# A fused decoder layer, its attention stage in another order: the context's maximum asked for between two query products, column sums one K/V tile later, the next batch element's transposes among the queries, the last products ahead of the layer norms

## What is computed

```
# 1: linear attention through one vector A per batch element
Xn = layernorm(x) * gamma + beta
Q, K, V = split(Xn @ W_in + b_in)
K, V = rotary(K), rotary(V)
A = 0.5 * sum over positions (K/|K| * V/|V|) + 0.5
x1 = layernorm(x + (A * Q) @ W_out + b_out + x)
# 2: product with ctx, both quantised to fp8 and back, scale = 448 / max|.|
x2 = layernorm(x1 + fp8(x1) @ fp8(ctx) + mask)
# 3: gated MLP (512 -> 2048 -> 512) plus 8 retrieved experts per token
out = layernorm(x2 + mlp(x2) + experts(x2))
```

## Time and profile before

| | us |
|---|---|
| median of 3 runs | 868.43 (864.55 to 869.49) |
| profiled execution: its own time | 864.76 |
| profiled execution: span of the instructions | 863.0 |
| TensorE busy | 790.3, 92% of the span |
| VectorE busy | 687.5, 80% |
| ScalarE busy | 298.0, 35% |
| GpSimd busy | 388.6, 45% |

### The profile page before, as it was taken

How to read it: one execution, slowest core, us unless ns; L and a number is a source line. 1 busy time by engine, 2 the same in 40 slices (tenths; PEclk the granted TensorE clock), 3 DMA queues, 4 the chain that set the end, 5 groups by cost and what they waited for, 6 DMA issues and landing times. The chain is left out here.

```text
span 863.0 us, 10406 instructions
## 1 busy us (share of the span) xinstructions
PE 790.3 (92%) x3510; PEld 639.1 (74%) x3510; DVE 687.5 (80%) x1329; ACT 298.0 (35%) x657; POOL 388.6 (45%) x308
## 2 busy tenths in 40 slices
PE   4988899998826899899999999999999999999994
PEld 3867688886704667688888888888877887887783
DVE  5658479874878687317777999999999999999997
ACT  5343335451134423221135342333333333333320
POOL 0231222221155423111247766776766766766431
PEclk9989899998965999999999999999999999999998
DMA  9464442576034202200002323232243233322113
GB/s 325 187 128 121 87 105 71 101 247 119 0 94 129 67 19 74 98 25 1 29 28 72 86 85 84 72 88 72 56 125 92 73 110 93 93 85 60 44 60 136
DMA packets 49510, 78.54 MB, mean 91 GB/s; under 512 B 17487, under 2 KB 26447, under 8 KB 48944
## 3 DMA queue, kind: packets, MB, share of 16 engines
q1 hardware_dynamic: 25600, 48.57, 16.7%
q0 software_dynamic: 22272, 29.29, 15.2%
q10 hardware_dynamic: 1584, 0.01, 0.1%
HBM read 107.29 MB, written 12.58 MB: 139 GB/s over the span
## 5 line engine op out<-in xcount | busy, mean ns | idle before, releaser
L1014 POOL TENSOR_TENSOR h_lo<-mid,h_hi 128x512 fp32r<-128x512 f32 x62 | 79.5, 1302 | 117.2 <-ACT h_hi L1134 112.3
L1144 ACT ACTIVATE gates<-dots 128x1 f32<-128x1 f32 x144 | 29.2, 203 | 232.1 <-DVE dots L1350 232.1
L1035 POOL DMA_INDIRECT ctx_q<-table_dram,row_i x64 | 80.6, 1259 | 62.0 <-DVE xall L1359 37.8
L1465 PE MATMUL gu<-x_hi,gate_hi 128*128 128x512 f32 x256 | 102.1, 399 | 3.2 <-DVE mid L1259 1.7
L1035 POOL DMA_INDIRECT scratch<-table_dram,row_i x64 | 82.7, 1293 | 39.5 <-issue 21.3
L1467 PE MATMUL gu<-x_hi,gate_lo 128*128 128x512 f32 x256 | 100.4, 392 | 0.0
L1466 PE MATMUL gu<-x_lo,gate_hi 128*128 128x512 f32 x256 | 100.4, 392 | 0.0
L1467 PE MATMUL gu<-x_hi,up_lo 128*128 128x512 f32 x256 | 99.6, 389 | 0.0
L1465 PE MATMUL gu<-x_hi,up_hi 128*128 128x512 f32 x256 | 99.6, 389 | 0.0
L1466 PE MATMUL gu<-x_lo,up_hi 128*128 128x512 f32 x256 | 99.6, 389 | 0.0
L1465 PE MATMUL ob<-down_hi,h_hi 128*128 128x512 f32 x248 | 97.5, 393 | 1.0 <-POOL h_lo L1014 1.0
(11 more groups left out here) (209 smaller groups left out, 1714.6 us busy)
## 6 DMA issues: line engine op xcount, KB each, us to landing
stage<-in_ctx SPq DMA_DIRECT2D x7, 1024.0 KB, 5.5
total<-prod POOLq DMA_DIRECT2D x12, 512.0 KB, 4.7
xall<-half_bo POOLq DMA_DIRECT2D x4, 1024.0 KB, 10.4
w_stage<-in_L_ffn_gate_w SPq DMA_DIRECT2D x8, 512.0 KB, 3.3
w_stage<-in_L_ffn_up_w SPq DMA_DIRECT2D x8, 512.0 KB, 3.4
w_stage<-in_L_ffn_down_w SPq DMA_DIRECT2D x8, 512.0 KB, 3.5
x_dram<-xall SPq DMA_DIRECT2D x4, 1024.0 KB, 4.9
x_tok<-x_dram SPq DMA_DIRECT2D x16, 256.0 KB, 3.5
```

The source lines that it names most:

```text
L1014: nc.gpsimd.tensor_tensor(lo[:, c], mid[c][:], hi[:, c].bitcast(F32), ALU.subtract).then_inc(hlo_done, 1)
L1035: nc.gpsimd.indirect_dma_start(rows[k], None, table_dram[:, :], bass.IndirectOffsetOnAxis(ap=row_i[t % 2][:, k:k + 1], axis=0), bounds_che ...
L1144: nc.scalar.activation(gates[:, t % 2, k:k + 1], dots[:, t % 2, k:k + 1], ACT.Silu).then_inc(gate_done, 1)
L1465: nc.tensor.matmul(dst, lhs[0], rhs[0], start=start, stop=False)
```

## The change

No arithmetic changes and no DMA is added. The order on three engines does, with the waits and the PSUM banks that it needs:

- TensorE: `token_sums(b-1)` goes behind K/V tile 1 (was: tile 0), `mix_sums(b-1)` behind tile 2 (was: tile 1). The first two transposes of the next element go ahead of the fourth query. `gather_largest(0)` goes between queries 0 and 1 and `spread(0)` behind query 1 (were: ahead of query 0, and behind it).
- The last element's four attention tiles use all four ob banks (were: two), and `gather_largest(1)` uses ob[2], after a wait for `residual` of tile 0.
- ScalarE: `squares(b, 1)` ahead of `copy_sums`, `high_y` (the high part of A*Q) behind `squares(b, 2)`, the first two scalings of the next x between queries 2 and 3, and for the last element `squares(3, 3)` ahead of query 0.
- VectorE: `multiplier` and `low_y` one K/V tile later; `products(0, 3)` behind the four `low` of the next element; `products(3, 3)` ahead of the four `finish_x1`.

```
# tensor
                     if b:
-                        for k in range(KC):
-                            key_value(b, 0, k)
+                        for i in range(2):
+                            for k in range(KC):
+                                key_value(b, i, k)
                         token_sums(b - 1)
-                        for k in range(KC):
-                            key_value(b, 1, k)
+                    for k in range(KC):
+                        key_value(b, 2, k)
+                    if b:
                         mix_sums(b - 1)
-                    for i in (2, 3):
-                        for k in range(KC):
-                            key_value(b, i, k)
+                    for k in range(KC):
+                        key_value(b, 3, k)
+                    query(b, 0)
                     if b == 1:
                         pe.wait_ge(amul_done, 1)
                         gather_largest(0)
-                    for c in range(KC):
-                        query(b, c)
-                        if b == 1 and c == 0:
-                            spread(0)
+                    query(b, 1)
+                    if b == 1:
+                        spread(0)
+                    query(b, 2)
                     if b == 1:
                         pe.wait_ge(scale_done, 1)
                     if b < LAST:
                         transposes(b + 1, 0)
                         transposes(b + 1, 1)
+                    query(b, 3)
# scalar
                     squares(b, 0)
+                    squares(b, 1)
                     if b:
                         copy_sums(b - 1)
-                    squares(b, 1)
-                    if b:
-                        for c in range(KC):
-                            high_y(b - 1, c)
...
                     squares(b, 2)
+                    if b:
+                        for c in range(KC):
+                            high_y(b - 1, c)
+                    if b == LAST:
+                        squares(b, 3)
                     query(b, 0)
                     query(b, 1)
-                    squares(b, 3)
+                    if b < LAST:
+                        squares(b, 3)
                     query(b, 2)
+                    if b < LAST:
+                        scaled_x(b + 1, 0)
+                        scaled_x(b + 1, 1)
                     query(b, 3)
                     if b < LAST:
-                        for c in range(KC):
-                            high(b + 1, c)
+                        high_x(b + 1, 0)
+                        high_x(b + 1, 1)
+                        high(b + 1, 2)
+                        high(b + 1, 3)
# vector
                         add_kv_bias(b, 1)
                         products(b, 0)
-                        multiplier(b - 1)
-                        for c in range(KC):
-                            low_y(b - 1, c)
...
                     add_kv_bias(b, 2)
                     products(b, 1)
-                    if b == 0:
+                    if b:
+                        multiplier(b - 1)
+                        for c in range(KC):
+                            low_y(b - 1, c)
+                    else:
                         low_wo()
...
+                    if b == LAST:
+                        products(b, 3)
                     if b >= 2:
                         for i in range(TB):
                             finish_x1(b - 2, i)
-                    products(b, 3)
+                    if 0 < b < LAST:
+                        products(b, 3)
...
+                    if b == 0:
+                        products(b, 3)
```

More of the change, by code:

```diff
@@ L330, in high_wo, with scaled_x @@
                     nc.scalar.activation(wo_hi[:].rearrange("p c n -> p (c n)"), stage[0][:], ACT.Copy).then_inc(wo_hi_done, 1)
-                def high(b, c):
+                def scaled_x(b, c):
                     j = KC * b + c
@@ L342, in high @@
                     nc.scalar.activation(xn_hi[:, c], xs[:, c % 2], ACT.Copy).then_inc(hi_done, 1)
+                def high(b, c):
+                    scaled_x(b, c)
+                    high_x(b, c)
                 def squares(b, i):
@@ L489, in scale_row @@
                     dve.wait_ge(amax_b, 2 * k + 1)
-                    own.did(nc.vector.tensor_reduce(arow[0:1, 0:1], ob[1][0:1, P:2 * P], AX.X, ALU.max))
+                    own.did(nc.vector.tensor_reduce(arow[0:1, 0:1], scale_bank[k][0:1, P:2 * P], AX.X, ALU.max))
                     own.wait()
@@ L546, in residual @@
                     dve.wait_ge(xb_in, 16 * (b + 1))
-                    nc.vector.scalar_tensor_tensor(tile(j), tile(j), 2.0, ob[2 + i % 2][:], ALU.mult, ALU.add).then_inc(z_done, 1)
+                    nc.vector.scalar_tensor_tensor(tile(j), tile(j), 2.0, att_bank(b, i)[:], ALU.mult, ALU.add).then_inc(z_done, 1)
                     dve.wait_ge(z_done, j + 1)
@@ L682, in gather_largest @@
                     pe.wait_ge(amax_t, k + 1)
-                    nc.tensor.transpose(ob[1][0:1, P:2 * P], amax1[:, 0:1], ident[:]).then_inc(amax_b, 1)
+                    nc.tensor.transpose(scale_bank[k][0:1, P:2 * P], amax1[:, 0:1], ident[:]).then_inc(amax_b, 1)
                 def spread(k):
                     pe.wait_ge(arow_done, k + 1)
-                    nc.tensor.matmul(ob[1][:, 2 * P:2 * P + 2], ones_row[:], arow[0:1, 0:2], start=True, stop=True).then_inc(amax_b, 1)
+                    nc.tensor.matmul(scale_bank[k][:, 2 * P:2 * P + 2], ones_row[:], arow[0:1, 0:2], start=True, stop=True).then_inc(amax_b, 1)
                 def transposes(b, c):
@@ L743, in query, with attention @@
                     last.then_inc(qt_mm, 1)
-                def attention(b, i, queried):
+                def attention(b, i):
                     hi, lo = y_of(b)
-                    if i >= 2:
+                    if b == LAST:
+                        if i < 2:
+                            pe.wait_ge(z_done, TB * (b - 1) + 3 + i)
+                        elif i == 3:
+                            pe.wait_ge(amul_done, B)
+                    elif i >= 2:
                         pe.wait_ge(z_done, TB * b + i - 1)
-                    elif queried is not None:
-                        pe.wait_ge(qt_out, KC * queried + 3 + i)
                     else:
-                        pe.wait_ge(z_done, TB * (b - 1) + 3 + i)
+                        pe.wait_ge(qt_out, KC * (b + 1) + 3 + i)
                     for k in range(KC):
@@ L796, in _ @@
                     if b:
-                        attention(b - 1, 0, b)
+                        attention(b - 1, 0)
                     if b < LAST:
@@ L803, in _ @@
                     if b:
-                        attention(b - 1, 1, b)
+                        attention(b - 1, 1)
                         if b == LAST:
                             mix_sums(LAST)
-                        attention(b - 1, 2, b)
-                        attention(b - 1, 3, b)
+                        attention(b - 1, 2)
+                        attention(b - 1, 3)
                 for i in range(TB):
-                    attention(LAST, i, None)
+                    attention(LAST, i)
                 pe.wait_ge(x1_done, TB)
@@ L817, in _ @@
                     last.then_inc(x1t_mm, 1)
+                pe.wait_ge(z_done, NT - 3)
                 gather_largest(1)
```

14 lines of the change are left out of this document (9 added, 5 removed).

## The result

| | before | after |
|---|---|---|
| median (range, runs) | 868.96 us (864.55 to 870.40, 4) | 854.17 us (853.68 to 855.75, 4) |
| ratio to before, 95% interval | | 0.983 (0.980 to 0.986) |
| profiled execution, its span | 864.76, 863.0 | 855.75, 853.9 |
| mean granted clock of the profile | 0.963 | 0.969 |

The change takes 14.8 us off the median; 14.0 was forecast for the gain and 853 for the time. The two profiled executions differ by only 9.0: the one of before is at the low end of its runs, the one of after at the high end.

A forecast was written before the change was run, and what follows sets the result against it. TensorE, 92% busy, bounds the kernel, with idle and low-clock stretches in the first block. Gains 10.8 (last column sums) + 3.5 - 0.3 = 14.0 take the profiled 864.76 to 850.8; median forecast 853, range 847.5 to 860.

The forecast's parts named there:

- third ctx load, landing: In b = 1: the load shares the engines with the accumulating bias DMA, landing 8.5 us after issue; bounds 5.0 and 11.2.
- transpose of the maximum: TensorE in b = 1, behind query (1,0): ctx's maximum out at 84.7, after 3.6 us idle (0.6 to 6) instead of 6.66.
- from there to (2,0): TensorE, maximum to K/V tile (2,0): 26.55 less 2.5 of low clock and 2.72 of moved query, 21.3 us.
- stall ahead of query (3,2): TensorE in b = 3: new wait of 3.0 us for query 2's bank, released by ACT, costing nothing by itself.
- sums to residual (2,3): Last column sums to attention (2,3)'s end: 10.7 us instead of 14.2 with the clock up, gain 3.5.
- if it stays up over 3.6 us idle: TensorE's clock ahead of ctx's maximum in b = 1: no fall in the shorter wait, saving 2.5 us.
- too short for a fall: b = 3, last column sums: 1.3 us of wait and 1.7 of tiny products leave the clock up; gain 3.5.
- Rival A: Clock falls in a new gap, at the maximum (2.5 us), b = 3 stall (1.2) or elsewhere: 856; chance 0.24.
- B: Third ctx load not slowed by the bias DMA, landing in 5.5 us: 3 us more gained, 850; chance 0.19.
- C: No gain: first block shorter, but the second block waits for something with its own date, 867; chance 0.05.
- D: Slower: clock falls at the b = 3 stall and stays low for 72 matmuls, 14.4 us, giving 870; chance 0.02.
- forecast's 5.5 of gain up to tile (1,3): TensorE in b = 1: tile (1,3) ends at 78.3 instead of 83.9 less 0.15, gain so far 5.5 us.

The follow-up runs named there:

- e10: The changed kernel again, no edit: 855.99 us, ratio 0.986 to the kernel before; its profiled execution took 852.97.
- e6: Changed kernel plus 18 useless matmuls in TensorE's gap between query (1,0) and the transpose of ctx's maximum: 855.51 us, ratio 0.984 to the kernel before.
- e1: The kernel before again, no edit: 869.05 us, ratio 1.0001.
- e2: Changed kernel with the accumulating bias DMA of b = 0 issued later, behind the first accumulating DMA of b = 1: 849.39 us, ratio 0.976 to the kernel before.
- e11: Changed kernel with column sums and mixing put back one K/V tile earlier, and ScalarE's copy of the sums ahead of the second squares: 862.90 us, ratio 0.993.
- e9: Changed kernel with the transpose of ctx's maximum put back ahead of query (1,0) and the broadcast behind it: 858.57 us, ratio 0.989 to the kernel before.
- e3: Changed kernel with squares (3,3) put back behind the emptying of queries (3,0) and (3,1) on ScalarE: 857.89 us, ratio 0.988 to the kernel before.
- e5: Changed kernel with products (3,3) put back behind the four finish_x1 of b = 1 on VectorE: 857.41 us, ratio 0.986 to the kernel before.
- e8: Kernel before plus only the early first two transposes, their scaling between queries 2 and 3, and products (0,3) behind the low parts: 869.26 us, ratio 0.9998.
- e7: Changed kernel with the bias DMA of b = 0 issued later and ctx's last quantising moved behind products (3,3): 845.13 us, ratio 0.974 to the kernel before.

## Why the prediction was right

*Step by step.* Against the forecast of 850.8 for the profiled execution it took 5.0 us more:

| step | forecast | after | why |
|---|---|---|---|
| K/V (1,0) | 52.5, clock up | 53.28, clock up | 0.6 of it in b = 0, whose first K/V tile had more slow matmuls in this run |
| first column sums | 64.6 | 64.95 | right |
| third ctx load, landing | 8.5 | 8.8 | right |
| transpose of the maximum | 84.7, 3.6 idle | 85.95, 4.33 idle | the late start and the landing |
| from there to (2,0) | 21.3 | 23.1 | the clock fell: 1.8 |
| (2,0) to (3,0) | 48.1 | 48.14 | right |
| stall ahead of query (3,2) | 3.0, by ScalarE | 2.86, by ScalarE | right |
| (3,0) to last column sums | 42.6 | 42.8 | right; 1.34 idle, 1.3 forecast |
| sums to residual (2,3) | 10.9 | 12.8 | the clock fell: about 2 |
| residual to x1's largest | 19.9 | 19.6 | as before; the 0.3 for slow small products was put here, but they stand behind x1's largest |
| from there to the end | 623.3 | 623.3 | right; x1's largest at 232.43, the execution 855.75 |

*The term that failed* is one, "if it stays up over 3.6 us idle" and its twin "too short for a fall" in b = 3: 1.8 and 1.9, 3.7 of the 5.0. The rows of before had shown falls about 4.6 us after work ended, and the forecast read that as a bound on the idle time. It was none: e10 has falls with idle times of 0.72, 2.52 and 2.87 us, e6 with 2.87, while after kept its clock over the same 2.86. Rival A had this mechanism and both places at which after's clock did fall: at the maximum (priced 2.5, measured 1.8) and at the last column sums (named without a price, measured 1.9). Its 856 is the time of the profiled execution, 855.75. Its price of 1.2 for a fall at the stall was too high by e10, and it did not name the place where most later profiles have a fall, the first column sums. The median of eight runs, 854.8, lies between rival A and the forecast. That the forecast's gain of 14.0 came out in the medians (14.8 in the first session, 12.8 in the second) is partly luck: its own sum has no new falls, and before pays for falls that its first profile did not show, as e1 has one at the first column sums. The order of waits and dates that it walked through did come, step by step; so the mechanism was right and the clock was not.

*The other rivals.* B, the load not slowed, fell: 8.8, and 5.2 once the bias DMA is elsewhere (e2). C, a second block with its own date, fell: from x1's largest to the end it is 623.3 in both profiles, and 1.6 less in e10's. D, slower, fell: each fall in the two profiles of the changed kernel's first block, up to x1's chain, was over in 3.4 us.

*Which part is worth what.* Undone singly: sums one tile earlier 8.1 (e11), maximum ahead of the query 3.8 (e9), squares behind the emptyings 3.1 (e3), products behind x1 2.6 (e5). Each is good to some 2 us, and the last is not clear of the noise. They add to 17.6 without the transposes, more than the whole change; that alone would be within the errors, but the transposes alone are worth 0.0 (e8), so the parts aren't independent. That the late sums are worth so much because the transposes bring TensorE to them earlier fits the 6.0 and 6.5 us that it stands idle ahead of them in e8 and e11. The forecast's 5.5 of gain up to tile (1,3) is the two together; in after it was 5.0.

*Left open.* Not tried by themselves: the late column sums on the kernel before, the changed kernel without the early transposes, the attention tiles' banks in b = 3, and the multiplier's new place on VectorE; the forecast gave the last two nothing. What decides between a fall and none at the same short wait was not found.

## What to carry to other kernels

- Move a wait together with what brings its engine there earlier. The early transposes alone only turned one wait into another, and without the late sums the change lost 8 of its 14 us.
- When loads are moved, look for another queue's DMA in flight at the new time. Here a 1 MB load went from 5.4 to 8.8 us, and issuing the unhurried transfer later gave 5.4 us, more than any part of the reordering but the late sums costs when undone.
- In front of a chain that ends at a date, look for long work that nobody waits for yet: the quantising step moved behind the products was worth 5 us for one line.
- Where the clock moves with short waits, take several profiles before a fall is called typical, or its absence.

## What the runs showed of the hardware

- At a wait of 0.7 to 2.9 us TensorE's granted clock sometimes fell to 1.2 GHz and sometimes did not, for the same instructions and the same wait to 0.01 us (the stall of 2.86 in after, 2.87 in e6 and e10). The waits of 0.7 to 1.2 us with a fall all stand ahead of 16 tiny products. A fall where TensorE's work is what counts cost 1.8 to 3 us; one ahead of a wait that TensorE had to sit out cost next to nothing (e10). Up to the last attention tiles every low stretch of the thirteen profiles lasted 3.4, 6.8 or 10.2 us, the longest where the wait at the sums was 4.5 to 6.5 us (e3, e8, e11).
- A 1 MB load of ctx landed in 8.8 to 9.3 us when it was issued 4 to 5 us behind a 1 MB accumulating DMA (seven profiles), and in 5.2 to 5.4 with that DMA elsewhere (e2, e7).
- The scatter of the kernel before from run to run, 864 to 873 us over 57 runs, goes with the mean granted clock, 0.951 to 0.965, by 4.3 us per 0.01. The version with the fewest waits (e7) repeats within 0.2 us in four runs of six.
